# Clipping the first attention's scores after their exponential, in SBUF, instead of before it, in PSUM

## What is computed

```
def _L0_xattn_ref(query, key_value, Wq, bq, Wk, bk, Wv, bv, Wo, bo):
    NUM_HEADS = 16; CLAMP = 10000.0        # head width 8
    ...
    attn = jnp.einsum('bhqd,bhkd->bhqk', q, k) * scale
    attn = jnp.clip(attn, -CLAMP, CLAMP)
    attn = jax.nn.softmax(attn, axis=-1)
    attn = jnp.where(jnp.any(jnp.isnan(attn)), 1.0 / Nkv, attn)
    x = jnp.einsum('bhqk,bhkd->bqhd', attn, v).reshape(B, Nq, Cq)
    return x @ Wo + bo
```

## Time and profile before

| | |
|---|---|
| median of 3 runs | 2078.24 us (2076.97 to 2085.89) |
| profiled execution, its own time | 2082.13 us |
| its span in the trace | 2080.4 us |
| rounds 4 to 31 of the first attention | 104.56 to about 282 us of the span |
| one round of these, mostly | 6.16 us |
| TensorE's granted clock, rounds 0 to 3 | 0.50 of full speed |
| TensorE's granted clock, 104 to 287 us | 0.96 |

### The profile page before, as it was taken

How to read it: one execution, slowest core, us unless ns; L and a number is a source line. 1 busy time by engine, 2 the same in 40 slices (tenths; PEclk the granted TensorE clock), 3 DMA queues, 4 the chain that set the end, 5 groups by cost and what they waited for, 6 DMA issues and landing times. The chain is left out here.

```text
span 2080.4 us, 40415 instructions
## 1 busy us (share of the span) xinstructions
PE 1827.4 (88%) x12306; PEld 1459.8 (70%) x12306; DVE 1514.7 (73%) x3109; ACT 1113.4 (54%) x2864; POOL 1179.7 (57%) x1243
## 2 busy tenths in 40 slices
PE   3687867799999999976999999997788887799998
PEld 2455546588888888865999999996544444588886
DVE  5688868677877778777666666665768786777876
ACT  1366645555555555543665656554346565555554
POOL 3666637467776677654333333334767773676764
PEclk9699976799999999986999999998879997699999
DMA  5111100456665555410000000000000000122222
GB/s 121 45 42 43 40 24 11 115 137 136 144 147 143 136 136 146 130 43 4 4 3 4 3 4 3 4 3 1 0 1 1 0 0 16 55 65 82 81 63 70
DMA packets 99991, 114.77 MB, mean 55 GB/s; under 512 B 18448, under 2 KB 55504, under 8 KB 99888
## 3 DMA queue, kind: packets, MB, share of 16 engines
q1 hardware_dynamic: 96960, 112.14, 21.2%
q10 hardware_dynamic: 2928, 1.39, 0.3%
HBM read 101.82 MB, written 3.28 MB: 51 GB/s over the span
## 5 line engine op out<-in xcount | busy, mean ns | idle before, releaser
L76 POOL TENSOR_TENSOR b_moe_hid_low<-b_moe_hid,b_moe_hid_high 128x512 fp32r<-128x512 f32 x256 | 331.4, 1295 | 172.4 <-ACT b_moe_hid_high L1027 168.7
L1033 ACT ACTIVATE bank<-bank 128x512 f32<-128x512 f32 x384 | 223.5, 582 | 341.0 <-PE bank L83 340.8
L1739 POOL TENSOR_TENSOR c_prob<-c_prob,c_recip 128x480 f32<-128x480 f32 x128 | 126.2, 986 | 307.5 <-DVE c_recip L1890 307.5
L1848 ACT ACTIVATE c_prob<-bank,c_shift 128x120 f32<-128x120 f32 x512 | 177.9, 360 | 182.1 <-DVE c_shift L1882 182.1
L1058 DVE TENSOR_TENSOR b_moe_gu<-bank,XC 128x512 f32<-128x512 f32 x256 | 176.7, 690 | 114.8 <-PE bank L83 99.0
L76 POOL TENSOR_TENSOR e_moe_hid_low<-e_moe_hid,e_moe_hid_high 128x512 fp32r<-128x512 f32 x128 | 165.5, 1293 | 84.2 <-ACT e_moe_hid_high L1027 83.4
L71 DVE CAST c_ts_high<-bank 128x480 fp32r<-128x480 f32 x128 | 85.0, 664 | 165.3 <-PE bank L1770 165.3
L1063 DVE TENSOR_TENSOR b_moe_hid<-bank,b_moe_gu 128x512 f32<-128x512 f32 x256 | 177.0, 691 | 8.9 <-POOL b_moe_hid_low L76 0.3
L1027 ACT ACTIVATE b_moe_hid_high<-b_moe_hid 128x512 fp32r<-128x512 f32 x256 | 159.7, 624 | 10.4 <-DVE b_moe_hid L1063 9.8
L1770 PE MATMUL bank<-c_cs,mT 96*128 96x120 f32 x1024 | 138.2, 279 | 6.0 <-POOL c_wvp_low L76 4.8
L1770 PEld LDWEIGHTS bank<-c_cs,mT 96*128 96x128 f32 x1024 | 132.6, 196 | 14.2 <-POOL c_wvp_low L76 5.2
(11 more groups left out here) (373 smaller groups left out, 5572.6 us busy)
## 6 DMA issues: line engine op xcount, KB each, us to landing
XC<-b_comb SPq DMA_DIRECT2D x256, 256.0 KB, 4.5
XC<-e_comb SPq DMA_DIRECT2D x64, 256.0 KB, 3.2
X<-in_x SPq DMA_DIRECT2D x4, 512.0 KB, 9.1
a_att_qs_high<-XC SPq DMA_DIRECT2D x32, 64.0 KB, 1.8
a_att_qs_low<-a_Q_low SPq DMA_DIRECT2D x32, 64.0 KB, 1.9
a_att_ks_high<-a_K_high SPq DMA_DIRECT2D x32, 64.0 KB, 1.9
a_att_ks_low<-a_K_low SPq DMA_DIRECT2D x32, 64.0 KB, 1.9
b_moe_w_gate<-in_b_wgT SPq DMA_DIRECT2D x8, 256.0 KB, 2.9
```

The costliest lines, as they stand in the source:

```text
L76: return eng.tensor_tensor(low.bitcast(F32R), x, high, ALU.subtract)
L1033: act.activation(gate_b[j % 4][:], gate_b[j % 4][:], ACT.Silu).then_inc(s_silu, 1)
L1739: pool.tensor_tensor(prob[k][:], prob[k][:], recip[:, k, :].unsqueeze(2).broadcast_to([P, HG, NKV]), ALU.mult).then_inc(s_norm, 1)
L1848: i = act.activation(prob[k][:, h, :], score_b[g % 2][:, h * NKV:(h + 1) * NKV], ACT.Exp, bias=shift[:, k, h:h + 1], accum_out=sums[:, k, ...
```

## The change

The turned scores are no longer clipped in PSUM. The shift matmuls follow the score matmuls without waiting for DVE. ACT takes the exponential of the unclipped, shifted scores into `probT`, and DVE clips the exponentials in SBUF (`clip`) between exp(-80) (1, where a NaN was found) and 1. To leave room for rounding above the maximum, a constant -8 (`LIFT`) rides along in row 8 of each group of `mz`. The product with the values waits for the two clips (`s_inA`, `s_inB`) where it waited for the second exponential. The causal attention of the last layer keeps its code. The core of the diff:

```
@@ gpsimd, start
+                        if clamp:
+                            pool.memset(mz[u][:].rearrange("p (g c) -> p g c", g=NG)[:, :, 2 * HG:2 * HG + 1], -LIFT)
@@ tensor, body
                         if has(t - 2):
-                            pe.wait_ge(s_inA, t - 1)
+                            if not clamp:
+                                pe.wait_ge(s_inA, t - 1)
                             pe.wait_ge(s_mrow, t - 1)
                             shift(u, (0, 1)).then_inc(s_shA, 1)
...
                         if has(t - 2):
-                            pe.wait_ge(s_inB, t - 1)
+                            if not clamp:
+                                pe.wait_ge(s_inB, t - 1)
                             shift(u, (2, 3)).then_inc(s_shB, 1)
                         if has(t - 3):
                             pe.wait_ge(s_vprep, t - 2)
-                            pe.wait_ge(s_expB, t - 2)
+                            if clamp:
+                                pe.wait_ge(s_inA, t - 2)
+                                pe.wait_ge(s_inB, t - 2)
+                            else:
+                                pe.wait_ge(s_expB, t - 2)
@@ vector
-                        dve.tensor_scalar(limit[:, 0:1], side_b[:, 0:1], 0.0, CLAMP, ALU.is_le, ALU.mult)
-                        dve.tensor_scalar(limit[:, 1:2], side_b[:, 0:1], 0.0, -CLAMP, ALU.is_le, ALU.mult).then_inc(s_limit, 1)
+                        dve.tensor_scalar(limit[:, 0:1], side_b[:, 0:1], 0.0, CLAMP - FLOOR + LIFT, ALU.is_le, ALU.mult)
+                        dve.tensor_scalar(limit[:, 1:2], side_b[:, 0:1], 0.0, LIFT - CLAMP, ALU.is_le, ALU.mult)
+                        dve.tensor_scalar(limit[:, 2:3], side_b[:, 0:1], 0.0, float(np.exp(-FLOOR)), ALU.is_gt, ALU.max).then_inc(s_limit, 1)
...
+                    def clip(u, half):
+                        both = probT[u][:, 2 * half:2 * half + 2, :]
+                        return dve.tensor_scalar(both, both, 1.0, limit[0:nk, 2:3], ALU.min, ALU.max)
...
-                        if has(t - 2):
+                        if clamp and has(t - 3):
+                            dve.wait_ge(s_expB, t - 2)
+                            clip(1 - u, 1).then_inc(s_inB, 1)
+                        if not clamp and has(t - 2):
                             dve.wait_ge(s_first, t + 1)
                             in_place(1).then_inc(s_inB, 1)
...
-                        if has(t - 1):
+                        if clamp and has(t - 2):
+                            dve.wait_ge(s_expA, t - 1)
+                            clip(u, 0).then_inc(s_inA, 1)
+                        if not clamp and has(t - 1):
                             dve.wait_ge(s_second, t + 1)
                             in_place(0).then_inc(s_inA, 1)
```

More of the change, by code:

```diff
@@ L43 @@
 A_SCALE = 8 ** -0.5
+LIFT = 8.0
+FLOOR = 80.0
 C_DH = 64
@@ L396, in attend_both_ways @@
                 anyodd = f32("anyodd", [P, 1])
-                limit = f32("limit", [P, 2])
+                limit = f32("limit", [P, 3])
             out_b, side_b = bank[6], bank[7]
@@ L652, in row_max @@
                                                  AX.X, ALU.max, negate=True)
+                    def clip(u, half):
+                        both = probT[u][:, 2 * half:2 * half + 2, :]
+                        return dve.tensor_scalar(both, both, 1.0, limit[0:nk, 2:3], ALU.min, ALU.max)
                     def in_place(half):
                         both = banks[0:nk, 2 + 2 * half:4 + 2 * half, :]
-                        if clamp:
-                            return dve.tensor_scalar(both, both, limit[0:nk, 0:1], limit[0:nk, 1:2], ALU.min, ALU.max)
                         both = both.rearrange("p b (h q) -> p (b h) q", h=HG)
@@ L2217, in constants @@
     row = np.arange(P) % 32
-    maxsel = ((row < 8)[:, None] & ((row % HG)[:, None] == np.arange(HG)[None, :])).astype(np.float32)
+    maxsel = ((row == 8)[:, None] | ((row < 8)[:, None] & ((row % HG)[:, None] == np.arange(HG)[None, :]))).astype(np.float32)
     d = np.arange(P) % 8
```

## The result

The changed kernel takes 2093.4 us (median of 10 runs, 2086.13 to 2098.86), the kernel before 2080.21 us beside it (10 runs, 2076.97 to 2085.89). The ratio is 1.0066 [1.0052, 1.0081]: 0.66% or 13.7 us slower. The forecast was 2084, with a range to 2091. It stood on 2078.24 us, the median of the first three runs of the kernel before. So 2.0 of the 9.4 us between forecast and result belong to that base, and 7.4 to the size of the change. The profiled execution of the changed kernel took 2096.69 us, the one of before 2082.13, which is 14.6 us less.

A forecast was written before the change was run, and what follows sets the result against it. The prediction took the chain from row maximum through clip B, `heads` and shift B to bound rounds: 28 x 0.22 = 6.2, + 0.15 start, - 0.6 end, 5.7 us longer, so 2084 us for the median, range 2075 to 2091.

The forecast's parts named there:

- The removed waits are worth nothing by themselves: PE's shifts A and B: their waits for the clips are not on the round's chain, so removing them gains nothing.
- Clip B is held by `qd_low`: On DVE: clip B in SBUF waits for POOL's `qd_low`, takes about 1.5 us and ends 0.56 us behind it.
- the low bound: DVE's clip in SBUF, unheld: 0.71 us for 1024 elements.
- 28 x 0.22 us: Rounds 4 to 31: the held clip B makes each round's chain 0.22 us longer, 6.2 us in all.
- What POOL pays: Clip B costs POOL 0.46 us a round; `kd_low` ends later within its cover, and clip A waits for it at no cost.
- the later start that was named as the sign: On POOL: `vh` should start near half a microsecond later after `qd_low` than before.
- The 0.7 us of cover: Time left between `kd_low`'s delayed end at 172.06 and PE's need of it for the next first phase at 172.78.
- Rounds 0 to 3 at nothing: The first rounds, with the clock at half: the change costs nothing there.
- The end: Round 33: clip B no longer waits for PE's phase and has no POOL beside it, a gain of 0.6 us.
- The sum of 5.7 us: Whole kernel: 6.2 us for 28 rounds, plus 0.15 at the start, minus 0.6 at the end, 5.7 us longer.
- the clock's rival: PE's granted clock falls more often as waits grow: five dips more, with the 5.7 us, make 2090.5; chance 0.10.
- The rivals of a fast or an unheld clip: Clip not held by POOL: fast, 2062, chance 0.07; or at its old rate, 2077 to 2078, chance 0.07.

The follow-up runs named there:

- after_accum: The changed kernel with clips that also write an accumulator output nobody reads; 2075.01 us, ratio 0.9987 against the kernel before.
- after_noA: The changed kernel without clip A, so the first half of the transposed exponentials isn't clipped; 2091.43 us, ratio 1.0076 against the kernel before.
- after_late: The changed kernel with clip B moved behind `heads` in DVE's program; 2084.6 us, ratio 1.0037 against the kernel before.
- before_warm: The kernel before with two matmuls of zeros a round at the end of PE's second phase; 2075.57 us, ratio 0.9986.
- after_warm: The changed kernel with four matmuls of zeros a round before PE's transpose of `heads`; 2080.56 us, ratio 1.0010 against the kernel before.

## Why the prediction was right and wrong

- **The removed waits are worth nothing by themselves: consistent.** Shift B still comes behind the transpose of `heads` (168.98 after 168.49). In `after_accum` the waits are gone as well, clip B is 0.07 us shorter than in PSUM (1.27 for 1.34), and the rounds are 0.05 us shorter (6.11 for 6.16). No run tried the waits alone.
- **Clip B is held by `qd_low`: right, and shown.** Forecast: starts 0.03 us behind, ends 0.56 behind, about 1.5 us. Measured: 0.03, 0.55, 1.56 us. `after_accum` takes the hold away at the same place and time, and 0.28 us a round go with it. The clip alone takes 0.74 us, near the low bound (0.71).
- **28 x 0.22 us: right.** Rounds at full clock went from 6.16 to 6.39 us, for 6.38 forecast. PE's wait for `heads` is 1.2 us, for 1.25 forecast.
- **What POOL pays, with clip A and `kd_low`: right in size.** `vh` went from 0.29 to 0.76 us, 0.47 for 0.46 forecast, though as a longer record and not as the later start that was named as the sign. Clip A takes 1.11 us, and PE's rounds don't wait for `kd_low`. `after_noA` shows no cost of clip A. The 0.7 us of cover is thin all the same: `after_late` used it up, and the wait appeared in 23 rounds.
- **Rounds 0 to 3 at nothing: right** (25.02 us in both).
- **The end: the right sign.** It is 3.1 us shorter for 0.6 forecast, but its time at the lower clock fell from 13.1 to 4.2 us. From before and `before_warm`, 1.6 us go with 6.2 us at that level, so 8.9 us less are worth 2.3 us, and 0.8 us remain for the clip.
- **The sum of 5.7 us: right, as far as it went.** With the clock held up in both kernels the change costs 5 us, give or take 4. The sum had no term for the clock; that stood only in the rival, and so the forecast was too low.
- **The step that failed is the weighing of the clock's rival**: "Against it: the wait grows only by 3% of a round. Chance 0.10." The direction and the mechanism stood in the text, but the number was wrong. Time at the lower clock between rounds 4 and 31 went from 14.5 to 59.1 us in the profiles. The rival had allowed for five more long rounds, each 1.3 us longer. There are six more: ten of the 27 distances are over 7.6 us, where four were 7.3 to 7.6. Three of the ten are 1.2 to 1.5 us longer than 6.39, about as in the rival, but seven are 1.8 to 2.1 us longer. The clock cost 12.1 us in the profiled executions, for 6.5 in the rival, and 8.7 us by the ratios. The 3% was the wrong measure. The wait is small against a round, but it is repeated in every round, and the kernel before had rounds in which the clock dipped already. In hindsight, a stage in which that happens should have given the rival an even chance, as a term added to the main mechanism and not as a case apart from it, and a price up to that of rounds that stay at the lower level (8.29 for 6.39 us).
- **The rivals of a fast or an unheld clip** did not come. The fast clip exists (0.74 us), but only where DVE asks ahead of POOL.

What stays open is why the granted clock falls in one round and not in the next of the same length. `after_noA` has the same round as the changed kernel at full clock, and 37.6 us at the lower level instead of 59.1. Its ratio is still as high (1.0076 lies inside the interval of 1.0066, and the reverse), and so is its loss of clock over all runs: a mean of 0.923 in four runs, for 0.922 in the changed kernel's ten. The profiled executions had 0.925 and 0.919. So a single profile doesn't tell a kernel's mean time at that level. That PE's idle time in front of the transpose matters is shown (`after_warm`, 59.1 to 4.0 us). How the time at the lower level depends on the length of that idle time was not measured.

## What to carry to other kernels

Before moving a VectorE operation from PSUM to SBUF, look in the trace at what GpSimd starts at the same event: here one that started 0.03 us earlier in every round turned a clip of 0.74 us into one of 1.56 us, and a slower form that GpSimd doesn't hold (1.27 us) was better. Ask whether the operation must be on the chain at all: moving it behind the instruction that PE waits for was worth 16 us in the old form, the clock's part among them, and together with the form that isn't held 24 us against the kernel before. Where the granted clock already dips in some rounds, a quarter of a microsecond more idle time of PE in each round can cost more through the clock than by itself, and the forecast's range has to reach to a stage that runs at the lower level.

## What the runs showed of the hardware that was not expected

- The clock reacted to little: PE's wait for `heads` grew from 1.0 to 1.2 us a round, and the time at 1.2 GHz within 27 rounds from 14.5 to 59.1 us in the profiles. Matmuls of zeros in that gap brought it to 4.0 us. In the kernels whose rounds are shortest (5.49 and 5.68 us) it is under 1 us. The Trainium skill, TensorE: Matmul & The Clock Gate, section "Part 1: The HAM clock gate", names the same two levels, 1.2 and 2.4 GHz, and the traces agree (0.51 and 1.00 in the two pieces above).
- A DVE instruction of 16 elements is held too: `mz` took 0.28 us, and 0.95 us beside `kd_low`, which it outlasted by 0.03 us (`after_late`).
- The hold works both ways by who asks first: `kd_low` took 1.51 us behind a clip, 0.98 without. Between two POOL instructions back to back (`qd_low` and `vh`) the waiting clip B gets its turn, in all 29 rounds of the changed kernel that have it 0.03 us behind `qd_low`.
- The accumulating form costs 1.27 us for 1024 elements and 0.08 us for its read, against 0.74 us for the plain form alone, and POOL's instructions beside it keep their length.
